# Edge lookups per partition of 18 sorted edges with four candidate nodes, and their three bf16 parts summed in PSUM

## What is computed

```python
ft = (feat @ W).reshape(n, H, OUT)              # H = 4 heads of 64
e_src = sum(ft * w_att_src, -1); e_dst = sum(ft * w_att_dst, -1)
e = leaky(e_src[src] + e_dst[dst], 0.2)
ex = exp(e - segment_max(e, dst)[dst])
a = ex / segment_sum(ex, dst)[dst] * dist
out = segment_sum(ft[src] * a, dst)

x = x + gnn(layernorm(x))
f = layernorm(x); w = softmax(f @ Wr + br)      # 8 experts
h = relu(bn(f @ W1[e] + b1)); h = relu(bn(h @ W2[e] + b2)); y_e = h @ Wo[e] + bo
x = x + sum_e w[:, e] * y_e
```

## Time and profile before

| | |
|---|---|
| time, median of 3 runs | 1559.56 us (1558.78 to 1561.06) |
| span of the profiled execution | 1556.4 us |
| TensorE busy | 1485.0 us, 95%, 8478 matmuls |
| VectorE busy | 1231.7 us, 79%, 2302 instructions |
| ScalarE busy | 742.2 us, 48% |
| GpSimd busy | 1063.0 us, 68% |
| transferred | 187.50 MB, of it 50 loads of 576 KB into `onehot_t` |

### The profile page before, as it was taken

One profiled execution on the slowest core, in us unless ns is written; L12 is line 12 of the kernel. 1 busy time (PEld: TensorE's weight loads), 2 busy tenths in 40 slices (PEclk: granted clock), 3 DMA queues, 4 the chain that ended last, 5 costly groups with the idle time before them and its releaser, 6 DMA issues.

```text
span 1556.4 us, 24165 instructions
## 1 busy us (share of the span) xinstructions
PE 1485.0 (95%) x8478; PEld 1298.3 (83%) x8478; DVE 1231.7 (79%) x2302; ACT 742.2 (48%) x1293; POOL 1063.0 (68%) x951
## 2 busy tenths in 40 slices
PE   6928999999999999999999999999999999999998
PEld 4727888878888888888888888888888888888887
DVE  7746787887788888878888888888888888888751
ACT  3500444444455555545555555554555555555543
POOL 4176767777778777777777877777777787787000
PEclk9959999999999999999999999999999999999999
DMA  8776344353543444353344444434334444443000
GB/s 239 203 233 192 110 137 124 106 141 94 144 121 111 122 126 127 103 142 108 103 135 118 112 119 118 128 106 137 108 107 134 119 111 119 129 111 91 18 7 8
DMA packets 106070, 187.50 MB, mean 120 GB/s; under 512 B 38357, under 2 KB 70490, under 8 KB 105919
## 3 DMA queue, kind: packets, MB, share of 16 engines
q0 software_dynamic: 44688, 123.13, 28.5%
q1 hardware_dynamic: 60701, 62.29, 13.9%
q10 hardware_dynamic: 560, 0.52, 0.1%
HBM read 172.72 MB, written 14.42 MB: 120 GB/s over the span
## 4 chain that ended last, share of the span: by engine, by line
PE 82%; DVE 9%; DMA 3%; issue 2%; ACT 2%; POOL 1%; SPq 0%; DVEq 0%; ACTq 0%
PE bankH L831 39%; PE bankY L860 21%; PE bankE L783 5%; PE bankE L784 5%; PE bankB L761 3%; PE bankE L776 2%; DVE gath L1431 1%; POOL gath L675 1%; DVE msg_lo L1437 1%; ACT h L1030 1%; DMA table<-gath 1%; PE bankA L808 1%; DVE x L1506 1%; DMA gath<-table,src_win 1%; PE bankA L799 1%
## 5 line engine op out<-in xcount | busy, mean ns | idle before, releaser
L675 POOL DMA_INDIRECT gath<-table,src_win x900 | 1042.5, 1158 | 336.0 <-issue 245.2
L1030 ACT ACTIVATE h<-bankH,bn_shift,bn_scale 128x250 f32<-128x250 f32 x800 | 400.9, 552 | 314.9 <-PE bankH L831 314.7
L831 PE MATMUL bankH<-h,w 128*128 128x250 f32 x1600 | 380.5, 380 | 2.8 <-ACT h L1030 2.1
L860 PE MATMUL bankY<-wo,h 128*125 128x256 f32 x1600 | 378.4, 379 | 1.1 <-DVE x L1506 1.1
L831 PE MATMUL bankH<-xT,w 128*128 128x250 f32 x1600 | 370.9, 374 | 0.3 <-ACT h L1030 0.3
L860 PEld LDWEIGHTS bankY<-wo,h 128*125 128x125 f32 x1600 | 296.1, 187 | 43.2 <-issue 1.4
L831 PEld LDWEIGHTS bankH<-h,w 128*128 128x128 f32 x1600 | 295.6, 191 | 43.4 <-issue 9.6
L831 PEld LDWEIGHTS bankH<-xT,w 128*128 128x128 f32 x1600 | 296.7, 190 | 32.2 <-ACT h L1030 0.4
L1437 DVE TENSOR_TENSOR msg_lo<-gath,msg_hi 128x2340 fp32r<-128x2340 f32 x90 | 234.3, 2603 | 88.0 <-ACT msg_hi L1002 88.0
L1002 ACT ACTIVATE msg_hi<-gath 128x2340 fp32r<-128x2340 f32 x90 | 193.8, 2154 | 217.0 <-PE bankE L784 192.0
L1506 DVE SCALAR_TENSOR_TENSOR x<-bankY,gate,x 125x256 f32<-125x256 f32 x400 | 173.9, 476 | 116.7 <-PE bankY L860 116.1
(11 more groups left out here) (190 smaller groups left out, 1027.6 us busy)
## 6 DMA issues: line engine op xcount, KB each, us to landing
onehot_t<-dst_low SPq DMA_DIRECT2D x48, 576.0 KB, 5.9
gath<-table,src_win POOLq DMA_INDIRECT x900, 2.9
x_res<-in_x SPq DMA_DIRECT2D x25, 250.0 KB
out<-x SPq DMA_DIRECT2D x25, 250.0 KB
table<-gath SPq DMA_DIRECT2D x25, 227.5 KB
w<-in_L_ffn_W SPq DMA_DIRECT2D x8, 512.0 KB
gath<-in_x SPq DMA_DIRECT2D x5, 672.0 KB
wo<-in_L_ffn_Wo SPq DMA_DIRECT2D x4, 512.0 KB
```

Source lines behind the costliest of these rows:

```text
L675: pool.indirect_dma_start(gath[:, g.slot(u), t, :], None, table, bass.IndirectOffsetOnAxis(src_win[:, g.win, u, t:t + 1], 0)).then_inc(row ...
L831: mm = pe.matmul(target[:, hc * 2 * NT:(hc + 1) * 2 * NT], weights[:, e * KC + c, hc * P:(hc + 1) * P], operand(c), start=(c == 0), stop=( ...
L860: mm = pe.matmul(bankY[0:NT, u * D:(u + 1) * D], h2[:, e % 2, c, u, :], wo[:, e * KC + c, :], start=(c == 0), stop=(c == KC - 1))
L1030: ins = act.activation(target[:, e % 2, hc, :, :].rearrange("p u n -> p (u n)"), source[:, hc * 2 * NT:(hc + 1) * 2 * NT], ACT.Relu, bias= ...
```

## The change

Since each node has a self loop and some 17 edges, the 18 consecutive edges of a partition reach few nodes. The new kernel looks at the partition's first edge: with its node n known, the edges of the partition belong to n, n + 1, n + 2 or n + 3 (`REACH` = 4). So the one-hot matrix is made for 128 first edges of a tile, not for 2304 edges; TensorE fetches the four candidates' scores for each partition, and VectorE picks among them for each edge.

- Prologue: `dst_low` and its stores and loads go. `edst_parts` is laid out as candidate, tile, part, head; SP copies it from SBUF to SBUF with its rows moved up by 1, 2 and 3 partitions (`parts_moved`), ahead of the weights. The flag also tells of any 18 consecutive edges that span more than 4 node numbers (`dst_next`, two more loads by POOL and two more operations by VectorE).
- `place` (VectorE) also computes each edge's distance from its partition's first edge, the first edges in bf16, and three masks (distance 1, 2, 3).
- `spread` (TensorE, behind `turn_bounds`): two matmuls write the first edges of both tiles to all partitions. `mark_first` (VectorE, ahead of `row_bounds`) compares them with the node number. `to_slots` (TensorE, one step later, between layer 1 and layer 2): for each tile three matmuls of 16 columns that add up the three parts in PSUM.
- `edge_sum` (VectorE, same place): copies candidate 0 to the 18 edges, then three `copy_predicated` with the masks.

```diff
+            def spread(a):
+                if a.begins(1):
+                    pe.wait_ge(t_rows, NP * 2)
+                    pe.wait_ge(rel_ready, 1)
+                else:
+                    pe.wait_ge(ed_ready, a.n)
+                for u in range(2):
+                    mm = pe.matmul(bankB[0:NT, u * P:(u + 1) * P], first_low[:, u:u + 1].broadcast_to([P, NT]), ident_low[:, :],
+                                   start=True, stop=True)
+                mm.then_inc(spread_done, 1)
+            def to_slots(a):
+                if a.begins(1):
+                    pe.wait_ge(parts_moved, 16 * (REACH - 1))
+                pe.wait_ge(mask_ready, a.n + 1)
+                for u in range(2):
+                    at = SLOT_AT + u * REACH * H
+                    for r in range(PARTS):
+                        mm = pe.matmul(bankB[:, at:at + REACH * H].rearrange("p (k h) -> p k h", h=H), first_mask[0:NT, u, :],
+                                       edst_parts[0:NT, :, a.tile(u), r, :], start=(r == 0), stop=(r == PARTS - 1))
+                mm.then_inc(edge_done, 1)
...
                     if a is not None and s == plan.bounds:
                         turn_bounds(f, a)
-                        for _ in small:
-                            pass
+                        spread(a)
+                    if a is not None and s == plan.rows + 1:
+                        to_slots(a)
...
 def place(a):
+                own.did(dve.tensor_tensor(offset[:], dst_win[:, a.win, :, :], dst_win[:, a.win, :, 0:1].broadcast_to([P, 2, TE]), ALU.subtract))
+                own.settle()
+                own.did(dve.tensor_copy(first_low[:], here[:, :, 0]))
+                own.did(dve.tensor_tensor(slot_mask[:].rearrange("p k u t -> p k (u t)"),
+                                          offset[:].rearrange("p u t -> p (u t)").unsqueeze(1).broadcast_to([P, REACH - 1, 2 * TE]),
+                                          iota[:, 1:REACH].unsqueeze(2).broadcast_to([P, REACH - 1, 2 * TE]), ALU.is_equal))
                 own.settle()
...
+            def mark_first(a):
+                dve.wait_ge(spread_done, a.n + 1)
+                dve.tensor_scalar(first_mask[0:NT].rearrange("n u e -> n (u e)"), bankB[0:NT, 0:2 * P], node[0:NT, 0:1], None,
+                                  ALU.is_equal).then_inc(mask_ready, 1)
+
             def edge_sum(a):
-                dve.wait_ge(edge_done, a.n * 2 + 2)
-                dve.tensor_reduce(ed[:].rearrange("p s t -> p (s t)"),
-                                  bankB[:, 0:PARTS * SEG * TE].rearrange("p (k c) -> p c k", k=PARTS), AX.X, ALU.add).then_inc(ed_ready, 1)
+                dve.wait_ge(edge_done, a.n + 1)
+                slots = bankB[:, SLOT_AT:SLOT_AT + 2 * REACH * H]
+                slots = slots.rearrange("p (u k h) -> p u k h", u=2, k=REACH)
+                each = ed[:].rearrange("p (u h) t -> p u h t", u=2)
+                own.did(dve.tensor_copy(each, slots[:, :, 0, :].unsqueeze(3).broadcast_to([P, 2, H, TE])))
+                for k in range(1, REACH):
+                    own.settle()
+                    ins = dve.copy_predicated(each, slot_mask[:, k - 1, :, :].unsqueeze(2).broadcast_to([P, 2, H, TE]),
+                                              slots[:, :, k, :].unsqueeze(3).broadcast_to([P, 2, H, TE]))
...
-                    if run and a is not None and s in (0, 2):
-                        make_onehot_t(a, s // 2)
...
                     if a is not None and s == plan.rows:
+                        mark_first(a)
                         row_bounds(a)
...
 # SyncE, ahead of the weights
-                load_dst_low(a + 1, 0)
-                load_dst_low(a + 1, 1)
+                sp.wait_ge(parts_ready, 1)
+                for k in range(1, REACH):
+                    sp.dma_start(edst_parts[0:NT, k, :, :, :], edst_parts[k:NT + k, 0, :, :, :]).then_inc(parts_moved, 16)
                 load_weights()
...
 # VectorE, prologue
                 if n == 10:
-                    dve.wait_ge(p_in, 32)
+                    dve.wait_ge(p_in, 64)
                     own.did(dve.tensor_tensor(scr[0:NT, :], dst_prev[0:NT, :], dst_all[0:NT, :], ALU.is_gt))
+                    own.did(dve.scalar_tensor_tensor(dst_next[0:NT, :], dst_next[0:NT, :].bitcast(I32), float(REACH - 1), dst_all[0:NT, :],
+                                                     ALU.subtract, ALU.is_gt))
```

More of the change, by code:

```diff
@@ L32 @@
 RING = 2
-LOW_AT = 12
 NORMS = 4
@@ L44 @@
 PARTS = 3
+REACH = 4
+SLOT_AT = 2 * P
 X_GROUPS = (0, 1, 2, 4, 6, 9, 12, 15, 18, 21, 25)
@@ L523, in body @@
                     load_window(sp, g + WINS)
-                if a is not None and (a + 1).within(NP):
-                    load_dst_low(a + 1, 0)
                 if g is not None and (g + 2).within(NP):
@@ L609, in _ @@
             load_window(pool, Pair(0))
-            pool.wait_ge(low_stored, 48)
-            for u in range(2):
-                load_low(pool, Pair(0), u)
             for r in range(FT):
@@ L758, in to_edges @@
                 for u in range(2):
-                    pe.wait_ge(onehotT_ready, a.tile(u) + 1)
-                    for t in range(TE):
-                        mm = pe.matmul(bankB[:, 0:PARTS * SEG * TE].rearrange("p (k s t) -> p k s t", k=PARTS, t=TE)[:, :, u * H:(u + 1) * H, t],
-                                       onehot_t[0:NT, u, t:WIN:TE], edst_parts[0:NT, :, a.tile(u) * H:(a.tile(u) + 1) * H],
-                                       start=True, stop=True)
-                        if t == TE - 1:
-                            mm.then_inc(edge_done, 1)
-                        yield
+                    mm = pe.matmul(bankB[0:NT, u * P:(u + 1) * P], first_low[:, u:u + 1].broadcast_to([P, NT]), ident_low[:, :],
[11 more added lines that the diff above has]
+                mm.then_inc(edge_done, 1)
             def aggregate(g, c):
@@ L870, in first @@
                 turn_bounds(None, a)
-                for pair in (a, a + 1):
-                    for _ in to_edges(pair):
-                        pass
+                spread(a)
+                to_slots(a)
             def body(f, g, a):
-                small = to_edges(a) if f is not None and a is not None else iter(())
                 plan = plan_of(g)
```

100 lines of the change are left out of this document (37 added, 63 removed).

## The result

| | before | after |
|---|---|---|
| time, median of 4 runs each | 1559.99 us (1558.78 to 1561.06) | 1520.68 us (1519.20 to 1523.71) |
| span of the profiled execution | 1556.4 us | 1518.4 us |
| TensorE busy | 1485.0 us, 8478 matmuls | 1437.3 us, 7778 matmuls |
| transferred | 187.50 MB | 158.55 MB |

A forecast was written before the change was run, and what follows sets the result against it. TensorE was taken to bound the steady part. 18 stages at 1.0 us (1.5 less 0.5), 3 us early, 0.9 lost at the end: together -20 us, to 1539.5 us; forecast bounds 1529 to 1551, range 1522 to 1556.

The forecast's parts named there:

- TensorE's own term: Steady stage: 36 matmuls (2.19) removed, `spread`, `to_slots` and one small-to-large change added; 1.5 us less (1.15 to 1.7).
- the wait at `turn_runs`: Step 0: longer `edge_sum` makes `runs` end later, so TensorE newly waits 0.5 us a stage (0.1 to 0.8).
- the second aggregation: Behind `to_slots`: its wait for `msg_lo`, which ends 0.14 us before TensorE starts, was claimed to stay covered.
- The early stages: Five stages, pairs 1 to 5: half the gain lost at `turn_runs`, 0.6 us each, 3 us gained (0 to 6).
- the start: Prologue: extra `dst_next` loads and `edst_parts` moves against removed loads and stores; put at 0, with 3 us either way.
- What the missing comparison gives back: VectorE, step 0: without `onehot_t`, subtraction to sum takes 0.46 us, not 0.82; 0.36 saved.
- rival (a): VectorE hides more: copies at lower bound, wait at `turn_runs` near 0.1; 35 us gained, 1524 us; chance 0.16.
- rival (c): VectorE loses 0.9 us more between `runs` and `mark_first`; TensorE stands at first aggregation or `to_slots`; 1556 to 1560; chance 0.11.
- the half that I had taken off for it: Early stages: TensorE already waits 10.8 us for VectorE at `turn_runs`, so half the gain there was counted lost.
- the last stage: Stage of the last aggregation: pays the longer `edge_sum` with nothing to save; 0.9 us lost.
- its margin at `to_slots`: Step 4: the mask from `mark_first` is ready 0.9 us before TensorE reaches `to_slots`, so no wait there.
- stages of 52.8 us: GpSimd's gathers are held by TensorE 2.9 us a stage, so POOL allows stages of 52.8 us and nothing below.

The follow-up runs named there:

- e1: The kernel before, its 36 `to_edges` matmuls taking 128 neighbouring columns of `onehot_t` as weights, not every 18th (lookup left wrong): 1529.02 us, ratio 0.9795.
- e3: The changed kernel without the three predicated copies, every edge taking candidate 0: 1518.19 us, ratio 0.9725.
- e6: The changed kernel with the three moves of `edst_parts` issued by ScalarE's queue behind `keep_bounds`, not by SyncE: 1517.92 us, ratio 0.9742.
- e2: The changed kernel with `first_mask` laid out with 8 bytes from column to column, where it was 2: 1524.88 us, ratio 0.9768.
- e9: The changed kernel without 16 of the 36 `msg_lo` matmuls for each pair, in chunks 2 and 3: 1509.54 us, ratio 0.9682.
- e7: The changed kernel with two unused 125 x 2048 bf16 comparisons put back on VectorE at steps 0 and 2: 1542.02 us, ratio 0.9890.

## Why the prediction was wrong in size

The place of the gain, the sign and the two engines that decide were right; the sizes were not. A steady stage gained 1.87 instead of 1.0. Of the 0.87 between them 0.32 is TensorE's own term, 0.36 the wait at `turn_runs` and 0.17 the second aggregation. Over 18 stages that is about 15 us. The early stages gave 6 us more than forecast and the start 4 us less.

**TensorE's term, the step that failed.** I had 1.5 us less a stage; it is 1.82. The error is in the sentence "`to_slots` is like the removed ones: 6 x 0.061". The 61 ns were read right and given to the wrong cause: I took them as the price of a small matmul. The code of `to_edges` takes a strided stationary operand, and the row with the load (165 ns) was in the trace to see. `to_slots` cost 0.15, not 0.37, `spread` 0.12, not 0.2. The second change between small and large matmuls cost 0.1 as forecast. The Trainium skill (TensorE: Matmul & The Clock Gate, section "Wait — 56ns, not 53.3ns?") names two floors for small matmuls, some 62 ns with hardware decode off and some 25 ns from start to start however small they are. That the 61 ns lie near the first is chance: the dense weights of e1 and of `to_slots` show 25 ns, the second, by which `to_slots` alone would by estimate have been costed at 0.15.

**The wait at `turn_runs`, the second step that failed.** Forecast 0.5 (0.1 to 0.8), measured some 0.14, near the edge of it. Of the 0.36 difference some 0.17 is `edge_sum` (1.25 for 1.42; a predicated copy 0.31 for 0.36) and 0.19 the copies of `logit`, 0.37 for 0.55, which no step of mine touched. What the missing comparison gives back was right: 0.46 from subtraction to sum, as forecast. So rival (a), VectorE hides more, is what happened at this place; in TensorE's term it was as wrong as the forecast (18 x 1.5, where 18 x 1.87 came). The shorter copies of `logit` are luck: nothing that I had costed makes them so. They go with the moment of a gather. In all 17 steady stages of the kernel before, and in e1, the issue of a gather begins 0.42 us ahead of them and they take 0.55; after, it begins 0.1 us or a little more behind their start and they take 0.35 to 0.41. No run moves the gather alone, so the cause stays open.

**The second aggregation** I had looked at only as something that stays covered. It wasn't covered before: TensorE lost 0.17 there in each stage, for `msg_lo`. The 1.8 us of waiting that I had read for the whole steady part don't hold this, since that view leaves out waits so short. I had seen that `to_slots` delays only TensorE there; what follows, that 0.17 of its cost falls into the old wait, I didn't draw. The rows were on hand, and I read the 0.14 between the two as slack, when it was the signal's way: after, the first matmul again starts 0.15 behind the end of `msg_lo` (795.76 to 795.91).

**The early stages.** Forecast 0.6 each, 3 us; measured 9.2 over five. TensorE's waits between 120 and 475 us, after (total, times, longest; before's first is in the earlier trace rows):

```profile
PE bankC L720 <- DVE suffix L1356: 10.6, 6, 5.0
PE bankB L749 <- DVE first_mask L1373: 4.1, 4, 1.8
```

The wait for the scan did not grow (10.8 before), so the half that I had taken off for it was not lost; and four waits at `to_slots`, 4.1 us, are new: rival (c) came true there and only there. In the steady plan that margin held. One part of the 9.2 is a clock that fell in the trace of before and not in that of after. The stretches from 350 to 360 us of that trace (length, then busy us of PE, PEld, DVE, ACT and POOL with their instructions, granted clock, DMA share, GB/s):

```profile
350.00:355.00 5.00, 5.00 (x49) 4.39 (x48) 4.86 (x8) 1.26 (x3) 3.17 (x2) 0.88 0.10 26
355.00:360.00 5.00, 5.00 (x25) 4.34 (x24) 1.64 (x6) 1.22 (x3) 2.89 (x4) 0.77 0.31 84
```

A granted clock of 1.00 is 2.4 GHz, and after has 1.00 in both stretches; 0.88 and 0.77 mean that the engine stood at 1.2 GHz for part of each. It had just waited 2.9 us for the scan and then done the small matmuls; after, the wait there is 2.2. By estimate that cost before some 5 x (0.12 + 0.23) = 1.75 us. It is not the old kernel's alone: the clock also fell in e1 (0.66 from 345 to 350 us) and in e3 (0.68 from 350 to 355), there behind a wait of 2.1, so why it fell stays open. In the steady part there is no such dip on either side. Five times 1.82, less the 4.1, with the 1.75 and the other waits (1.6 less for `msg_lo`, 0.6 more for `messages`), makes about 8 of the 9.2; where the rest comes from no run tells.

**The start and the end.** I put 0 with 3 us either way for the start; it lost 4.05. Some 2.5 of this is that the moves stand among the weights (taking them out in e6 gave 3.0); I had seen that they stand there, but counted the loads that they replace against them; the 1.5 of the later first gather comes in e1 too, with the old prologue, and is not put to the change. For the last stage I had 0.9 lost; its interval shrank by 0.9: the stage that I meant still saves its `to_edges`, so I was off by one there. `mark_first` took 0.48, not 0.42, and its margin at `to_slots` held in the steady part, as forecast.

**GpSimd.** I wrote that POOL allows stages of 52.8 us and nothing below. e2 has the same stage as the kernel after, while POOL waits 36.6 us for TensorE between 600 and 1400 us in e2 and 1.8 in the other. By my reckoning that would make 51.3 the least stage in the one and 53.7 in the other, and e9 came to 53.24. So a stage less POOL's waits is no floor, and no run here shows where it lies.

## What to carry to other kernels

Before a duration is taken from a row for another operation, look at the row's operands: two matmuls of the same size differed by 2.4 times, because one took its weights with a step. Weight loads have rows of their own; a load that is longer than others of its shape is worth a test of its own. Here that test, one index, showed 32 of the 39 us. It also shows how little the lookup by candidates adds by itself, some 7 or 8 us, as long as dense weights could be had otherwise. And where a change moves work from a full engine to one with 0.1 us of slack, count everything that leaves that engine on the same stretch: the comparison that went is what paid for the copies that came. And work put in front of a wait that is already there costs less than its length.

## What the runs showed of the hardware

- A load of 128 bf16 columns as weights took 96 ns dense (e1; 97 in the kernel after), 116 ns with columns 8 bytes apart (e2) and 165 ns with 36 (before); the step from one small matmul to the next was 25, 32 and 61 ns.
- A predicated copy of 128 x 144 fp32 from PSUM under a uint8 mask took 0.31 us in a dependent chain, a plain copy of the same shape 0.30.
- A comparison of 125 x 256 fp32 from PSUM, written as bf16, took 0.48 us dense (after) and 0.79 with the results 8 bytes apart (e2).
- A gather's issue beside the bf16 comparison takes longer. GpSimd's timeline of before, where the comparison runs from 785.84 to 786.65:

```profile
784.20 0.95 POOL L675 DMA_INDIRECT gath<-table,src_win  x1 [0.30 <-issue]
785.45 1.32 POOL L675 DMA_INDIRECT gath<-table,src_win  x1 [0.30 <-issue]
```

In e7 the gather that meets the comparison put back at 779.30 takes 1.46. The Trainium skill (SBUF — State Buffer, section "Who interferes with whom") says that VectorE in its two-port modes and GpSimd lock each other out of a port pair they share. The traces agree: 0.37 to 0.51 us more for a gather under a comparison of 0.75 to 0.81.
- Three moves within SBUF of 146.5 KB each took 12.9 us to land with weight loads of 512 KB right behind them (after), counted from the last one's issue; in e6, ahead of the weights, at most 6.3 (83.0 to 89.25).
